# Normalised y in an SBUF buffer, outer products kept whole, and a reordered fill in a macaron transformer kernel

## The reference

```python
x = x + 0.5 * ffn(layernorm(x))
x = x + attn(layernorm(x))
x = x + 0.5 * ffn(layernorm(x))

def ffn(x):      # 512 -> 64, 16 hidden units for each of the 64, -> 64 -> 512
    s = x @ Win + bin_
    h = relu(s[..., None] * W1 + b1)
    g = (h * W2).sum(-1) + b2
    return g @ Wout + bout

def attn(x):     # 16 heads of 32 channels
    q, k, v = split(x @ w_attn)
    q, k = elu(q) + 1, elu(k) + 1
    # causal linear attention, S_t = S_(t-1) + k_t v_t^T, z_t = z_(t-1) + k_t
    y = (q_t S_t) / (q_t . z_t + 1e-6)
    return y @ w_proj
```

## Time and profile before

| what | value |
|---|---|
| three runs | 2327.67 us median (2326.47 to 2327.98) |
| the profiled execution | 2329.01 us, of it span 2327.3 us |
| PE, PEld busy | 97%, 76% |
| DVE, ACT, POOL busy | 83%, 62%, 36% |
| granted TensorE clock, mean | 0.989 |

### The profile page before, as it was taken

How to read it: one execution, slowest core, us unless ns; L and a number is a source line. 1 busy time by engine, 2 the same in 40 slices (tenths; PEclk the granted TensorE clock), 3 DMA queues, 4 the chain that set the end, 5 groups by cost and what they waited for, 6 DMA issues and landing times.

```text
span 2327.3 us, 74160 instructions
## 1 busy us (share of the span) xinstructions
PE 2266.8 (97%) x32210; PEld 1770.7 (76%) x32210; DVE 1935.2 (83%) x3393; ACT 1438.7 (62%) x2310; POOL 846.0 (36%) x871
## 2 busy tenths in 40 slices
PE   5899999999999999999999999999999999999997
PEld 3677777777777777777777777777777777777775
DVE  6888888889888889888889888889888889887767
ACT  6755657555657556657556656556656656666556
POOL 6333333433243433333333243434234333333312
PEclk8999999999999999999999999999999999999997
DMA  6001101111101111101111111111111111111111
GB/s 179 20 21 38 56 21 57 57 56 38 57 21 57 56 57 38 57 21 57 57 57 38 45 32 57 57 54 41 39 39 57 57 50 45 39 39 38 39 32 44
DMA packets 50215, 111.62 MB, mean 48 GB/s; under 512 B 8801, under 2 KB 10849, under 8 KB 45794
## 3 DMA queue, kind: packets, MB, share of 16 engines
q1 hardware_dynamic: 49890, 106.87, 15.1%
HBM read 72.25 MB, written 34.60 MB: 46 GB/s over the span
## 4 chain that ended last, share of the span: by engine, by line
PE 79%; DVE 13%; POOL 3%; issue 3%; ACT 2%; DMA 0%; DVEq 0%; SPq 0%; POOLq 0%; ACTq 0%
PE bank L1370 33%; PE att L1370 18%; PE att L1407 6%; PE att L1485 5%; PE att L1510 5%; PE att L1427 3%; DVE st L901 2%; DVE acc_psum L963 2%; PE att L1501 2%; PE bank L1436 2%; PE bank L1473 2%; POOL A L449 1%; DVE yl L931 1%; PE bank L1453 1%; DVE res L976 1%
## 5 line engine op out<-in xcount | busy, mean ns | idle before, releaser
L567 ACT ACTIVATE xhat<-res,nmr,rstd 128x512 f32<-128x512 f32 x384 | 298.4, 809 | 324.9 <-DVE nmr L909 266.7
L588 ACT ACTIVATE ffr<-ffs,b1c,w1c 128x512 f32<-128x512 f32 (+3 forms) x576 | 437.9, 781 | 27.9 <-DVE acc_psum L963 21.7
L453 POOL TENSOR_SCALAR_AFFINE_SELECT A<-A 128x512 f32<-128x512 f32 x256 | 156.6, 635 | 724.1 <-ACT A L540 724.1
L963 DVE SCALAR_TENSOR_TENSOR acc_psum<-ffr,w2c,acc_psum 128x512 f32<-128x512 f32 (+3 forms) x540 | 385.4, 714 | 32.4 <-ACT ffr L588 7.5
L442 POOL TENSOR_TENSOR res<-res,hbout 128x512 f32<-128x512 f32 x256 | 353.9, 1403 | 0.4 <-ACT xhat L567 0.4
L449 POOL TENSOR_TENSOR A<-qT,A 128x512 f32<-128x512 f32 x128 | 192.3, 1514 | 244.6 <-DVE zc L1005 102.2
L901 DVE BATCH_NORM_STATS2 st<-res 128x6 f32<-128x512 f32 x384 | 261.5, 681 | 9.5 <-DMA res<-in_L_attn_x_dram 3.7
L1370 PE MATMUL att<-xh,wa_h 128*128 128x512 f32 x648 | 260.4, 402 | 1.5 <-DVE xl L931 1.5
L1370 PE MATMUL att<-xh,wa_l 128*128 128x512 f32 x648 | 256.7, 396 | 0.0
L1370 PE MATMUL att<-xl,wa_h 128*128 128x512 f32 x648 | 256.7, 396 | 0.0
L1370 PE MATMUL bank<-wa_h,xh 128*128 128x512 f32 x512 | 218.7, 427 | 0.0
(11 more groups left out here) (135 smaller groups left out, 5060.6 us busy)
## 6 DMA issues: line engine op xcount, KB each, us to landing
xf<-scratch SPq DMA_DIRECT2D x128, 256.0 KB, 4.3
res<-in_L_attn_x_dram SPq DMA_DIRECT2D x31, 1024.0 KB, 5.3
out_dram<-res SPq DMA_DIRECT2D x31, 1024.0 KB, 4.3
scratch<-rden SPq DMA_DIRECT2D x128, 8.0 KB, 1.7
res<-in_L_attn_x_dram SPq DMA_DIRECT2D x4, 256.0 KB, 3.7
kT<-in_L_attn_w_attn_dram SPq DMA_DIRECT2D x1, 1024.0 KB, 5.7
qT<-in_L_attn_w_attn_dram SPq DMA_DIRECT2D x1, 1024.0 KB, 9.6
v<-in_L_attn_w_attn_dram SPq DMA_DIRECT2D x1, 1024.0 KB, 12.0
```

The lines of the kernel that those rows point to most:

```text
L453: eng.affine_select(out=A[:, h, :, :], in_=A[:, h, :, :], compare_op=ALU.is_ge, fill=0.0, base=0, pattern=[[0, 4], [1, P]], channel_multip ...
L567: eng.activation(xhat[t % 2][:, :], res[b % SLOTS][:, t, :], ACT.Identity, bias=nmr[:, n, b % 2, t:t + 1], scale=rstd[:, n, b % 2, t:t + 1 ...
L588: eng.activation(ffr[i % 2][p, w], ffs[p, w], ACT.Relu, bias=b1c[p, i:i + 1], scale=w1c[p, i:i + 1]).then_inc(s_hr, 1)
L963: eng.scalar_tensor_tensor(psum[p, w], r[p, w], w2c[p, i:i + 1], psum[p, w], ALU.mult, ALU.add).then_inc(s_hm, 1)
```

## The change

- VectorE writes normalised y into a new SBUF buffer `yn`. `ysplit` reads it on both engines, and the four banks are free (`emptied("sc")`) when `ynorm` is done (`s_yn`). `ynorm` now also waits for the previous tile's `yl`.
- TensorE's order: `outer(j, 0)` and `outer(j, 1)` no longer surround `attend`; `outer(j, 0)` stands whole between `scores(j, 2)` and `attend(j, 2)`, `outer(j, 2)` after `attend(j, 3)`. `values(j, 3)` is cut in two by `scores(j, 1)`. `key(j, 2)` stands right ahead of `scores(j, 2)`. Of the denominators, `den(j, 0)` stays, and 1 to 3 move behind the first part of `ff_in`. `update(j, 3)` moves behind `ff_out(j, 0)`. The orders of ScalarE, VectorE and GpSimd and the banks are changed with it.
- The fill: bout comes by a broadcasting DMA and is scaled on GpSimd; the small constants are loaded by ScalarE's queue ahead of its first `normalise`; w_attn's k part is loaded right after Win; w_proj ahead of `win` and block 2. GpSimd rounds w_attn's k and q parts and Wout, ScalarE the v part and w_proj, and the low parts are made in quarters (16 steps in all, `WPLO`), with other work in between.
- `hidden` of a block that runs alone uses four relu buffers, made of the halves of the two.

```diff
+        yn = sb("yn", [P, 4, P])
@@
-            return {"v": s_v, "xT": s_xTl, "y": s_x2, "sc": s_yl}[kind], 4 * b + i + 1
+            return {"v": s_v, "xT": s_xTl, "y": s_x2, "sc": s_yn}[kind], 4 * b + i + 1
@@
-        WALO = {1: 1, 0: 2, 2: 3}
+        WALO = {1: 4, 0: 8, 2: 12}
+        WPLO = 16
@@ sync
-            eng.dma_start(bout_st[0:1, :], bout.rearrange("(a n) -> a n", a=1)).then_inc(s_bout, 16)
             wa_v = w_attn.rearrange("(k p) n -> p k n", p=P)
             eng.dma_start(wa_st[1][:, :, :], wa_v[:, :, C:2 * C]).then_inc(s_wa[1], 16)
+            eng.dma_start(hbout[:, :], bout.rearrange("(a n) -> a n", a=1).to_broadcast([P, C])).then_inc(s_bout, 16)
@@ gpsimd
+            def weights_lo(n, k):
+                w = slice(n * C, n * C + C)
+                e.wait_ge(*{1: (s_wkh, 1), 0: (s_wkh, 2), 2: (s_whi, 1)}[n])
+                eng.tensor_tensor(wa_l[:, k, w], wa_st[n][:, k, :], f32(wa_h[:, k, w]), ALU.subtract).then_inc(s_walo, 1)
@@ gpsimd, a round
                 if on(j):
                     zsum(j, 1)
+                if on(j + 2):
+                    bias(1, j + 2, 1)
+                if on(j):
                     zsum(j, 2)
                     zsum(j, 3)
...
                     mask(j, 2, 2)
+                if on(j - 1):
+                    bias(0, j - 1, 3)
+                if on(j + 2):
+                    bias(1, j + 2, 3)
@@ scalar
-                copy(yh[o][:, :, :], att[:, :, 0:P], s_yh)
+                copy(yh[o][:, :, :], yn[:, :, :], s_yh)
@@ vector
                 e.wait_ge(s_rs, 64 * (b + 1))
-                eng.tensor_tensor(att[:, :, 0:P], att[:, :, 0:P], rs[:, :, t * P:t * P + P], ALU.mult).then_inc(s_yn, 1)
+                e.wait_ge(s_yl, 4 * b + t)
+                eng.tensor_tensor(yn[:, :, :], att[:, :, 0:P], rs[:, :, t * P:t * P + P], ALU.mult).then_inc(s_yn, 1)
@@
-                lo_part(yl[o][:, :, :], att[:, :, 0:P], yh[o][:, :, :], s_yl)
+                lo_part(yl[o][:, :, :], yn[:, :, :], yh[o][:, :, :], s_yl)
@@ vector, a round (as it is after): ynorm 0, hidden 5 and 6, ysplit 0, hidden 7, mask(j, 1, 1), mask(j, 1, 3), ...
@@ tensor, a round
                     den(j, 0)
+                if on(j - 1) or on(j + 2):
+                    ff_in(j, 0)
+                if on(j):
                     den(j, 1)
                     den(j, 2)
                     den(j, 3)
-                if on(j - 1) or on(j + 2):
-                    ff_in(j, 0)
...
                     values(j, 3, 0)
+                    scores(j, 1)
                     values(j, 3, 1)
-                    scores(j, 1)
                 if on(j + 1):
                     channels(j + 1, 0)
                 if on(j):
-                    outer(j, 0, 0)
                     attend(j, 1)
                     update(j, 1)
-                    outer(j, 0, 1)
                     key(j, 2)
                     scores(j, 2)
-                    outer(j, 1, 0)
+                    outer(j, 0, 0)
+                    outer(j, 0, 1)
                     attend(j, 2)
                     update(j, 2)
-                    outer(j, 1, 1)
                 if on(j + 1):
                     channels(j + 1, 1)
                 if on(j):
+                    outer(j, 1, 0)
                     scores(j, 3)
-                    outer(j, 2, 0)
+                    outer(j, 1, 1)
...
                     attend(j, 3)
                 if on(j + 1):
                     channels(j + 1, 2)
                 if on(j):
+                    outer(j, 2, 0)
                     outer(j, 2, 1)
```

More of the change, by code:

```diff
@@ L201, in carried, with relu_of @@
             return 4 * (b // PER * (PER - 1) + b % PER) + g + 1
+        def relu_of(j, i):
+            w = columns(j)
+            o = BLK // 2 * (i // 2 % 2) if alone(j) else 0
+            return ffr[i % 2][halves(j), w.start + o:w.stop + o]
         def hid(j, i):
@@ L735, in _ @@
                 if j == 0:
-                    hidden(-1, 9)
                     hidden(-1, 10)
                     hidden(-1, 11)
+                if on(j):
+                    key(j, 0)
+                if j == 0:
                     hidden(-1, 12)
                 if on(j):
-                    key(j, 0)
+                    values(j, 0)
                 if j == 0:
@@ L812, in _ @@
                     channels(j + 1, 1)
+                if on(j - 1) or on(j + 2):
+                    hidden(j, 15)
+                if j == NB - 1:
+                    flipped(0, j, 0)
+                if on(j + 1):
+                    channels(j + 1, 2)
                 if j == NB - 1:
                     normalise(L3, j, 1)
[L815 to L818 removed]
                 if on(j):
@@ L832, in _ @@
                     hidden(NB, 0)
+                    hidden(NB, 1)
+                    hidden(NB, 2)
+                    hidden(NB, 3)
+                if on(j + 1):
+                    channels(j + 1, 3)
                 if on(j) and updates(j, 3):
@@ L869, in _ @@
                     hidden(NB + 1, 3)
+                if on(j) and j < NB - 1:
+                    normalise(L3, j, 3)
+                if j == NB - 1:
                     hidden(NB + 1, 4)
@@ L1198, in _ @@
                 if on(j - 1) or on(j + 2):
+                    hidden(j, 8)
                     hidden(j, 9)
+                if on(j):
+                    ynorm(j, 1)
                 if on(j + 1):
@@ L1227, in _ @@
                 if on(j):
-                    mask(j, 3, 1)
-                if on(j - 1) or on(j + 2):
-                    hidden(j, 13)
-                if on(j + 1):
-                    channels(j + 1, 1)
+                    ynorm(j, 3)
                 if j == NB - 1:
@@ L1303, in _ @@
                     stats_of_sum(L2, j + 2, 3)
+                if on(j + 3):
+                    shift(L1, j + 3)
+                if on(j) and j < NB - 1:
+                    transposed(0, j, 0)
+                if j == NB - 1:
+                    hidden(NB, 7)
+                    hidden(NB, 8)
+                if on(j) and j < NB - 1:
+                    transposed(0, j, 1)
                 if j == NB - 1:
@@ L1532, in outer @@
                     op.then_inc(s_po, 1)
-            e.wait_ge(s_bout, 16)
-            e.wait_ge(s_const, 7)
-            o = take("bout", 0, 0)
-            eng.matmul(o[:, :], tri[0:1, :], bout_st[0:1, :], start=True, stop=True).then_inc(s_mbout, 1)
             for t in range(TILES):
```

432 lines of the change are left out of this document (206 added, 226 removed).

## The result

The changed kernel takes 2392.99 us (median; 2386.85 to 2397.63) for 2327.19 before on the same chip, or 66 us more; the estimated ratio is 1.0275, 95% interval 1.0261 to 1.0289. The forecast was 2340 us, its range 2302 to 2362. The direction was right, the size wrong by a factor of five. The profiled execution is one of the longer ones: it has a span of 2395.9 us, 68.6 above that of before.

The account below looks back on a forecast made before the run. The prediction took TensorE's instruction list to bound the kernel. From 2329.0 us it added 25 for rounds 1 to 30, less 11 for the fill and 1 for the tail: 2342, as a median 2340, range 2302 to 2362.

Parts of the forecast that it names:

- The late denominators: Moving `den` 1 to 3 delays reciprocal, DMAs and `ynorm`, so TensorE waits: +1.15 us a round, between +0.3 and +1.7.
- VectorE is back in step by the third tile: After the second tile's late masks, VectorE has caught up by the third tile; no further lateness was priced there.
- TensorE's list: TensorE's reordered matmuls, with waits before the third `attend` and `ff_out` removed: -0.3 us a round, between -0.5 and +0.1.
- the buffer: `ynorm` and `ysplit` on SBUF instead of PSUM: 0 to +0.3 us each on VectorE, taken as 0.
- the fill: Start up to the first projection, -4 us, and round 0, -7: together -11 us, between -17 and +1.
- The cover of the writes: Time between the denominators' DMA writes landing and the reads' issue: between 0 and 1.37 us, taken as 0.5.
- The step on the second `attend`: TensorE waits 0.85 us more for the second tile's masks, which stand behind the late `ynorm` on VectorE.
- The step on the second scores: The second scores start 0.1 us late, about 0.5 in even rounds: 0.3 on the mean.
- the reads come in time: Rival: the denominators' DMA reads land early enough that the wait for `ynorm` nearly vanishes: 2307 us, chance 0.29.
- the last parts no longer wait for GpSimd: In the moved denominators, a saving between 0 and -0.2 us a round, taken as -0.15.
- the lock: Rival: `yl` of the second tile waits for GpSimd's addition on shared SBUF ports, 1 us a round: 2370 us, chance 0.08.
- the fill gives little: Rival: ScalarE's DMA issues delay the first normalise, denominators bind round 0: fill -2 us, 2349 us in all, chance 0.13.

Follow-up runs that it names:

- run 2: The kernel before with only the last three parts of the denominators moved behind the first part of `ff_in`: 2379.24 us, ratio 1.0214.
- run 13: run 10 with the last three parts of the denominators behind the first part of `ff_in` again: 2388.02 us, ratio 1.0260.
- run 10: The changed kernel with the denominators put back and the end and beginning of a round ordered as in the kernel before: 2340.36 us, ratio 1.0048.
- run 4: The changed kernel with the second tile's masks ahead of `ysplit(j, 0)` and `hidden(j, 7)` on VectorE, their score copies ahead of `hidden(j, 7)` on ScalarE: 2386.08 us.
- run 1: The changed kernel with the last three parts of the denominators ahead of the first part of `ff_in` again: 2366.23 us, ratio 1.0161.
- run 5: run 1 with the beginning of a round in the old order on ScalarE, VectorE and GpSimd: 2369.59 us, ratio 1.0174.
- run 9: run 1 with the end of a round, VectorE's list behind `outer(j, 3)`, in the old order: 2369.61 us, ratio 1.0177.
- Run 7: The kernel before with the buffer `yn` alone, no order changed: 2337.01 us, ratio 1.0033.
- run 15: Run 7 with GpSimd's additions moved behind the second tile's masks, the last one behind the third's: 2330.70 us, ratio 1.0011.
- run 11: run 10 with the three edits of run 6 and run 8 on top: 2333.25 us, ratio 1.0020.
- run 6: run 5 with `update(j, 3)` ahead of `ff_out(j, 0)` again: 2368.91 us, ratio 1.0170.
- run 8: run 6 with the edit of run 3, and ScalarE's `key(j, 2)` ahead of `score(j, 2, 0)`: 2369.01 us, ratio 1.0172.
- run 3: The changed kernel with the first half of the first tile's `outer` moved between `update(j, 1)` and `key(j, 2)`: 2404.64 us, ratio 1.0318.

## Why the prediction was wrong

The sum failed in five terms. The late denominators were priced at 34 us and cost 48 to 51. "VectorE is back in step by the third tile" put at nothing what is 12 us. TensorE's list was to give 9 us and gave about none, the buffer was priced at 0 and costs 8, the fill was to give 11 and gave 2.

**The late denominators.** The mechanism was right in each link, and the term too small: +1.15 us a round (34 us) for 1.6 to 1.7 (48 to 51 us, runs 2 and 13). The lateness of `ynorm` was put at 1.0 us; behind the start of `attend` on v it comes at 3.21 us in odd rounds and 3.51 in even ones, for 1.66, so it is 1.55 to 1.85 late. The cover of the writes was sized well: over the rounds of before, they land 0.54 to 0.62 us ahead of the reads' issue (I took 0.5). What failed is what I held fixed. The writes land 4.2 us after their first issue, for 3.8. It is the last of the four that is slow: it lands 2.9 us after its own issue in the mean, for 1.4 before, and so it does in runs 2 and 13, where the denominators are late too (3.2 and 2.9), but not in run 10 (1.5). Why is open. The reads' last landing is 7.1 to 7.3 us after the first read's issue, for 6.9 to 7.0, though the four are now issued within 1.3 us and not 1.9. I moved the issue, and didn't ask whether the transfers' own time would stay. In even rounds the slack before `ynorm` was also smaller than the 0.5 us of round 13: 0.3 in the mean. The step on the second `attend` was good (0.85 forecast, 0.76 and 0.93 measured; run 4 shows that it is VectorE's order). The step on the second scores was not: 0.3 forecast, 0.8 to 0.9 measured, which the larger lateness explains. The rival that the reads come in time is refuted.

**"VectorE is back in step by the third tile"** failed. The third scores are 0.25 to 0.7 us late, by something that I didn't have in the sum: the gaps inside the groups of small matmuls (last section), 0.4 us a round in the changed kernel, 12 us.

**TensorE's list.** "The only waits of a normal round that I see the change remove" was true and worth less than its sum. With `sums` in time, `ff_out` starts without its wait, and its last part then waits 0.3 us (in odd rounds) for the bank that VectorE's first addition frees: the 0.32 were not gone but late by three parts. For even rounds I had +0.2 for the update within `ff_out`; it is 0.67, as the same bank is late there too. By these rows my -0.3 a round came out near 0. The denominators came out a little better than forecast (their two parts take 1.15 us together, for 1.22 and 1.29; +0.05 was the forecast), but "the last parts no longer wait for GpSimd" was wrong as a reading of what the move saves. They would have waited 0.5 to 0.9 us longer, since the ends and beginnings of the rounds, whose moves I had read as neutral, made the sums late (runs 1, 5, 9, 10). This costs nothing in the changed kernel, but it hides half of what undoing `den` would bring.

**The buffer.** Priced at 0, with the lock as a rival of 0.08. Run 7 has it at 8 us, run 15 shows the lock as the cause of 6. The row that decides was there; I set it aside by an argument about which engine asks first. The Trainium skill (SBUF — State Buffer, section "SBUF: two separate sides") calls the shared pair an exclusive lock that the first holds for its whole instruction; run 7's row agrees, with 0.55 us of `yl` left after the addition's end. The place differs from the one I named: it is the first tile's `yl`, and it was shown in the old order; what the lock costs in the changed kernel was not measured.

**The fill.** -11 forecast, -2 in the trace. The first projection starts at 41.67 us, not near 37 (41.25 before):

```profile
13.59 1.89 POOL L426 CAST wa_h<-kT 128x2048 fp32r<-128x2048 f32 x1 [4.51 <-DMA kT<-in_L_attn_w_attn_dram]
...
41.67 0.77 PE L1388 MATMUL att<-xh,wa_h 128*128 128x512 f32 x1 [1.50 <-DVE xl L939]
```

k's weights came 3.7 us earlier, as expected, but it is `xl` that the first projection waits for, and it waits 1.5 us for it, as before. I had followed the weights because GpSimd waited 8 us for them, though TensorE didn't. The rival "the fill gives little" came true in its size. Of its reasons, ScalarE's first normalise does start later (9.38 us for 5.97), but its fourth ends only 0.8 us later, and what holds round 0 was not tested. The tail, -1 forecast, is +1 together with round 31.

**The sum by what was measured.** Run 10 is 12 us above before: the buffer, the middle with its gaps and `ff_out`, less the fill; the edits of run 11 take 7 of these back. The denominators' place adds 48 (run 13), the ends and beginnings of the rounds the last 5, which the intervals don't resolve: 65 us in all.

## What to carry to other kernels

A round trip through DMAs that ends 0.5 us ahead of its reader is no slack but the bound itself: moving its start by 2 us behind other work costs nearly all of it (1.55 to 1.85 us here), and here once more through VectorE's list, where the next tile's masks stand behind the reader. When a wait is removed, find who is late next before booking the gain, and when an edit gives nothing, try it again where the other wait is gone (runs 6 and 8 against run 11). Two late things at the same place hide each other: only undoing both, or each in turn with the other undone (runs 1, 10, 13), gives their prices.

## What the runs showed of the hardware

TensorE seems to run out of instructions. In the changed kernel 132 small matmuls, each with its weight load, follow each other without a full-size one (second `attend`, `update`, `key`, third scores). In 13 of 28 rounds a gap of 0.55 to 1.8 us stands inside one of these groups, put down to "issue" (a 14th is in the update behind them). The DMA records have a queue of 16 KB pieces marked instruction. One piece moves just ahead of the end of round 13's gap, between 1042.5 and 1044.1 us (queue, packets, MB, share of the engines):

```profile
q8 instruction: 1, 0.02, 5.6%
```

Over the traces of twelve kernels, from 199 to 2300 us, there are 69 places inside a group of small matmuls where one starts 0.54 us or more after the last and the wait is put down to "issue", and TensorE resumes in each of them 1.2 to 1.6 us after the end of such a piece, though these come only every 9 us (254 in the changed kernel). Six full-size matmuls (1.4 us) amid the small ones take most of them away: 14 to 1 in run 3, 9 to 2 from run 10 to run 11. That the piece is what TensorE waits for is inferred from this timing and from these edits. The Trainium skill (Runtime: NRT & Kernel Launch, section "Instruction fetch mechanics") says that instructions come in blocks of 16 KiB and that crossing a block is "mostly hidden"; here it isn't, 12 us in the changed kernel, where small matmuls stand this dense.
